# Two half-blocks of an inner layer as steps of their own, and a new table of places for the whole order

## The reference, cut to what matters

```python
x = x + 0.5 * ffn(layernorm(x))
x = x + attention(layernorm(x))
x = x + 0.5 * ffn(layernorm(x))

# ffn, weights ternary: 256 -> 1024 (twice) -> 1024 -> 1024 -> 256
h = silu(lin(x, w1)) * lin(x, w2)
h = gelu(lin(h, h1))
h = gelu(lin(h, h2))
return lin(h, w3)

# attention: 16 heads; each row looks at 24 rows at fixed offsets 0 ... 768 before it
scores = einsum('bhnd,bhnod->bhno', q, k_g) * scale + pos_bias
out = einsum('bhno,bhnod->bhnd', softmax(scores), v_g)
return out_flat * sigmoid(x @ Wgate + bgate) @ Wout + bout
```

## Time and profile before

| | |
|---|---|
| median of 3 runs | 1610.91 us (1610.43 to 1613.33) |
| profiled execution | 1609.98 us, span 1608.1 us |
| PE busy | 1528.4 us (95% of the span) |
| DVE busy | 1086.0 us (68%) |
| ACT busy | 677.6 us (42%) |
| POOL busy | 553.3 us (34%) |
| mean granted TensorE clock | 0.987 |

### The profile page before, as it was taken

The page is one execution under the profiler, slowest core; times in us unless marked ns, Lnnn a source line. Parts: engine busy times, 40 slices in busy tenths (PEclk is TensorE's granted clock), DMA queues, the critical chain, the costliest instruction groups (busy, mean ns, idle before and its releaser), DMA issues.

```text
span 1608.1 us, 19160 instructions
## 1 busy us (share of the span) xinstructions
PE 1528.4 (95%) x6978; PEld 1224.9 (76%) x6978; DVE 1086.0 (68%) x1475; ACT 677.6 (42%) x1062; POOL 553.3 (34%) x402
## 2 busy tenths in 40 slices
PE   7689999999999999999999999999999999998998
PEld 6567888777777778787777877768788877786887
DVE  6323758894777686777876877778675978793322
ACT  7434445344343435344534353434343444352442
POOL 2003051535171607162526070533614245434020
PEclk9899999999999999999999999999999999999999
DMA  7662848666766494857765757557474776754332
GB/s 308 252 241 101 281 140 302 224 207 226 232 234 218 155 312 142 279 171 262 261 229 183 251 182 261 185 192 254 157 265 158 269 247 223 269 198 157 118 100 71
DMA packets 189218, 342.41 MB, mean 213 GB/s; under 512 B 15552, under 2 KB 138560, under 8 KB 188736
## 3 DMA queue, kind: packets, MB, share of 16 engines
q1 hardware_dynamic: 189120, 341.13, 62.1%
HBM read 319.05 MB, written 30.41 MB: 217 GB/s over the span
## 4 chain that ended last, share of the span: by engine, by line
PE 66%; DVE 12%; POOL 8%; DMA 7%; ACT 4%; issue 3%; SPq 0%; DVEq 0%; POOLq 0%; ACTq 0%
PE f_bank L1101 22%; PE f_bank L1102 22%; PE a_banks L1179 6%; PE f_bank L1030 4%; PE f_bank L1031 4%; DMA weights_hi<-in_ffn_w 3%; POOL acc L693 3%; PE f_bank L1130 2%; PE f_bank L1131 2%; DVE slot L935 2%; DVE slot L979 2%; DVE S L941 2%; POOL acc L690 2%; PE a_banks L1199 1%; POOL h_lo L707 1%
## 5 line engine op out<-in xcount | busy, mean ns | idle before, releaser
L1101 PE MATMUL f_bank<-h_hi,wring 128*128 128x512 f32 x2048 | 824.4, 403 | 31.1 <-POOL h_lo L707 12.4
L1102 PE MATMUL f_bank<-h_lo,wring 128*128 128x512 f32 x2048 | 813.6, 397 | 0.0
L1101 PEld LDWEIGHTS f_bank<-h_hi,wring 128*128 128x128 f32 x2048 | 387.6, 189 | 131.9 <-issue 18.4
L1102 PEld LDWEIGHTS f_bank<-h_lo,wring 128*128 128x128 f32 x2048 | 387.6, 189 | 93.2 <-issue 1.4
L773 ACT ACTIVATE h_hi<-f_bank,colv 128x512 fp32r<-128x512 f32 x256 | 176.5, 689 | 553.1 <-PE f_bank L1102 552.9
L895 DVE TENSOR_TENSOR h_lo<-f_bank,h_hi 128x512 fp32r<-128x512 f32 x256 | 175.2, 687 | 258.5 <-ACT f_bank L774 256.8
L707 POOL TENSOR_TENSOR h_lo<-f_gated,h_hi 128x512 fp32r<-128x512 f32 x128 | 165.4, 1305 | 449.1 <-ACT h_hi L767 448.3
L1030 PE MATMUL f_bank<-fT_hi,w_in 128*128 128x512 f32 x480 | 197.5, 411 | 11.6 <-ACT f_gated L762 5.4
L1031 PE MATMUL f_bank<-fT_lo,w_in 128*128 128x512 f32 x480 | 191.5, 399 | 0.0
L979 DVE TENSOR_TENSOR slot<-slot,a_banks 128x1280 f32<-128x1280 f32 (+4 forms) x124 | 169.5, 1375 | 21.1 <-DMA slot<-keys_and_values 20.7
L935 DVE TENSOR_TENSOR slot<-slot,a_banks 128x1280 f32<-128x1280 f32 (+4 forms) x124 | 170.5, 1375 | 17.0 <-DMA slot<-keys_and_values 16.8
(11 more groups left out here) (117 smaller groups left out, 1328.1 us busy)
## 6 DMA issues: line engine op xcount, KB each, us to landing
wring<-weights_hi SPq DMA_DIRECT2D x256, 512.0 KB, 4.6
slot<-keys_and_values SPq DMA_DIRECT2D x128, 384.0 KB, 4.9
slot<-keys_and_values SPq DMA_DIRECT2D x64, 640.0 KB, 4.0
slot<-keys_and_values SPq DMA_DIRECT2D x312, 128.0 KB, 4.4
slot<-keys_and_values SPq DMA_DIRECT2D x64, 256.0 KB, 5.7
weights_hi<-in_ffn_w SPq DMA_DIRECT2D x16, 512.0 KB, 5.0
keys_and_values<-kv_out SPq DMA_DIRECT2D x32, 256.0 KB, 2.3
xf<-in_x SPq DMA_DIRECT2D x8, 512.0 KB, 5.8
```

The costliest lines, as they stand in the source:

```text
L1101: pe.matmul(bank[:, :], hi, h_hi[src][:, k, :], start=(k == 0), stop=False)
L1102: last = pe.matmul(bank[:, :], hi, h_lo[src][:, k, :], start=False, stop=(not general and k == KH - 1))
```

## The change

h(l,0) and h(l,1) are split into four steps: `f_begin` 0 and 1 (turns 0 to 5 of block 0, of block 1) and `f_hidden` 0 and 1 (turns 6 and 7). The matmuls and their order among each other stay as they were; an attention step may now stand at any of the three seams where before it had to stand in front of or behind h(l,0). As the plan of h(l,1) now begins with its `f_begin`, its weight block and, in pass 0, the copy of it are due 3.7 earlier in planned time. And the numbers of the table are new: six of the 14 `TIMES`, most of `FOLLOW`, ten of the 16 `STARTS`.

```diff
-TIMES = [4.5, 9.5, 11.8, 13.4, 16.0, 24.8, 22, 3.8, 5.6, 53.0, 58.4, 3.1, 87.5, 3.5]
+TIMES = [3.5, 9.5, 11.8, 14.3, 16.9, 29.3, 21.6, 3.8, 5.6, 53.0, 58.8, 3.1, 88.4, 3.8]
-FOLLOW = dict(silu=-1.5, gate=0.1, cut=1.9, low=2.0, gelu=-0.6,
-              lo=0.9, residual=-1.3, residual2=0.4, fill=20.7, stats=-0.6, turn=4)
+FOLLOW = dict(silu=-1.5, gate=0.1, cut=1.9, low=2.7, gelu=-1.0,
+              lo=1.0, residual=-0.9, residual2=0.1, fill=23.1, stats=-0.7, turn=4)
-STARTS = [70, 149, 219, 312, 386, 453, 537, 617,
-          688, 768, 847, 925, 1006, 1087, 1158, 1236]
+STARTS = [73, 149, 219, 312, 381, 448, 537, 618,
+          690, 769, 851, 918, 1007, 1087, 1158, 1236]
...
+    ABREAST = 2
...
                 for layer in range(2):
+                    for m in range(ABREAST):
+                        pe(2.8, "f_begin", r, layer, m)
                     for m in range(KH):
-                        done = pe([6.5, 0.95, 3.7][min(m, 2)], "f_hidden", r, layer, m)
+                        done = pe(0.95 if m < ABREAST else 3.7, "f_hidden", r, layer, m)
+                        if m < ABREAST:
+                            begin["f_hidden", r.j, layer, m] = begin["f_begin", r.j, layer, m]
...
-                if general or m > 1:
-                    part(m, 0, KH)
-                elif m == 0:
-                    part(0, 0, EARLY)
-                    part(1, 0, EARLY)
-                    part(0, EARLY, KH)
+                if general:
+                    if not early:
+                        part(m, 0, KH)
+                elif early:
+                    part(m, 0, EARLY)
                 else:
-                    part(1, EARLY, KH)
+                    part(m, EARLY if m < ABREAST else 0, KH)
```

More of the change, by code:

```diff
@@ L1082, in bank_free, with run_hidden @@
                     pe.wait_ge(f_tlo, r.at(2, m - TURN_AT - 1))
-            def run_hidden(r, layer, m, ring, general):
+            def run_hidden(r, layer, m, early, ring, general):
                 src = (r.p + layer) % 2
@@ L1207, in run @@
                     "f_in": lambda r, m: run_in(r, m, ring, general),
-                    "f_hidden": lambda r, layer, m: run_hidden(r, layer, m, ring, general),
+                    "f_begin": lambda r, layer, m: run_hidden(r, layer, m, True, ring, general),
+                    "f_hidden": lambda r, layer, m: run_hidden(r, layer, m, False, ring, general),
                     "f_out": lambda r: run_out(r, ring, general),
```

## The result

| | before | after |
|---|---|---|
| median | 1611.01 us (20 runs, 1606.67 to 1614.85) | 1615.07 us (20 runs, 1609.43 to 1620.78) |
| profiled execution | 1609.98 us, span 1608.1 | 1611.20 us, span 1609.4 |
| mean granted clock, profiled | 0.987 | 0.990 |

The ratio is 1.0027, interval 1.0016 to 1.0038: the change made the kernel 4 us slower. The prediction said 1601, faster, with 1612 as its upper end.

A forecast was written before the change was run, and what follows sets the result against it. It took TensorE's own work, unchanged, plus its stands to bound the kernel. Gains less the losses in passes 5 and 10 summed to -9.5 us, giving 1601 us; own range 1596 to 1607, 8 in 10 for 1593 to 1612.

The forecast's parts named there:

- Pass 11, f_in: In pass 11's f_in, s11 starting earlier removes TensorE's 2.80 us stand and the lower clock behind it: -4.3 us.
- Pass 0, weight blocks: In pass 0, copies 8 and 9 go out together, fill 9 leaves 3.4 us earlier, all kept: -3.4 us.
- Waits for `a_hat`: TensorE's waits for `a_hat` shrink because `stats` is planned 1.0 earlier against `turn`: -2.8 us.
- Pass 9, layer 1: At h(1,4), TensorE comes 1.5 us later and f_lo(1,2) is done 0.8 earlier, ending stand and lower clock: -3.6 us.
- DVE's `h_lo` in passes 4, 5 and 10: TensorE's remaining waits for DVE's layer 1 input in these passes go: -2.4 us.
- Pass 10, layer 0: POOL's sums and `f_low` end later, TensorE stands 4.6 us before `a_z_turn` with lower clock after: +4.1 us.
- pass 5: In layer 0, the same pattern as pass 10 with s4 and s5, including one lower clock stretch: +3.5 us.
- Pass 6: One TensorE wait for `a_z` goes, as s5 starts 5 earlier: -0.6 us.
- Clock: After each long TensorE stand the granted clock falls to its lower level, charged at 1.6 us per stand.
- `a_stats` among the products: Rival: between products 3 and 4 in passes 5 and 10, `a_stats` costs 4.9 us each; about 1611, chance 0.17.
- SP's queue: Rival: earlier fills hold up key and value loads, 1.2 us in each of 13 attention passes; 1616, chance 0.18.
- The seam is free: Rival: sums in passes 5 and 10 start no later, so both loss terms fall away; -17.1, 1594 us, chance 0.17.

The follow-up runs named there:

- lo12_ahead: Changed kernel with DVE's f_lo(1,2) planned 1.7 us earlier; 1611.95 us, ratio to before 1.0007.
- gate_back: Changed kernel with the gate projection back at 24.8 us after a subblock's start instead of 29.3; 1612.52 us, ratio to before 1.0017.
- all_stands_out: Changed kernel with f_lo(1,2) 1.7 us earlier, in passes 4 and 9 its gelu and f_lo another 2.8, s11's statistics 2 us later; 1608.65 us, ratio 0.9987.
- stats_back: Changed kernel with the planned time of stats back from 3.5 to 4.5; 1616.54 us, ratio to before 1.0043.
- s4s5_back: Changed kernel with the starts of s4 and s5 back at 386 and 453; 1615.61 us, ratio to before 1.0034.
- copy_back: Changed kernel with copy 9 in pass 0 put back behind fill 8; 1616.09 us, ratio to before 1.0039.
- stats11_later: Changed kernel with the statistics of s11 planned 2 us later; 1614.23 us, ratio to before 1.0028.
- stats11_and_low2: Changed kernel with s11's statistics planned 2 us later and f_low 2 of pass 10 planned 0.3 us earlier; 1615.45 us, ratio to before 1.003.
- s10_back: Changed kernel with the start of s10 back at 847 instead of 851; 1618.5 us, ratio to before 1.0039.

## Why the prediction was wrong, by its own steps

*Pass 11, f_in (-4.3).* Right: -4.8 in the changed kernel, -4.6 with s11's start alone.

*Pass 0, weight blocks (-3.4).* The mechanism was right: the second fill went out 1.23 us behind the first (1.20 was said). The sum's "they are kept" failed: -1.8 in the profile. The 3.6 us at fill 10 are down to 1.8 at fill 15, as each later copy took longer from its issue to the fill. The experiments put the pair at 1 to 3 us.

*Waits for `a_hat` (-2.8, beside s11's 2.0).* They fell from 6.1 to 2.5 us, by 3.6 of the 4.8. But the step priced only what left. The operation moved is DVE's `a_stats`, and what it is moved past was not looked up: in passes 2 and 12 it went ahead of f_lo(1,2), and h(1,4) stood 1.25 and 2.23 us. lo12_ahead got this back, 3.1 us.

*Pass 9, layer 1 (-3.6), and DVE's `h_lo` in passes 4, 5 and 10 (-2.4).* This is the step that failed most. They said that no wait for DVE's `h_lo` would be left; 9.4 us are, a miss of 9.4 us in the sum. "f_lo(1,2) is done 0.8 us earlier" was read off DVE's order alone. f_lo needs the gelu, and that stands on ScalarE behind `a_tanh` and f_scale, since the gate moved to 29.3; gate_back and all_stands_out show it. Counted from the start of layer 1 in pass 9, TensorE did come to h(1,4) later, by 1.9 us (1.5 was said for the gate's work), but f_lo(1,2) began 1.8 us later too, and the stand went from 2.04 to 1.91 us. Pass 9's 1.8 us in the profile are luck: the half clock of 3.4 us that followed before did not follow. With the four long stands of h(1,4) out, all_stands_out is 6.4 us below the changed kernel, at 0.9987 of before (0.9973 to 1.0001).

*Pass 10, layer 0 (+4.1) and pass 5 (+3.5).* The new stands are where they were said (3.96 us in f_in 6 of pass 10, 2.47 and 2.71 us in f_in of pass 5), but between f_in 0 and layer 1 both passes are only 1.6 us longer in the profile. The reckoning through GpSimd's chain was good to 1.2 us, with T as there the start of pass 10's f_in: the first sum began at T + 3.2 (3.8 was said), `f_low` 7 ended at T + 32.7 (33.9), `a_z_turn` came at T + 38.9 (39.8), h(0,3) at T + 44.6 (45.7). POOL was idle for 0.8 us between that first sum and `f_low` 7. What failed is the clock's part, 1.6 us charged behind a stand of 4.6 us in front of `a_z_turn`. The lower clock came earlier, for 6.8 us in f_in, so TensorE reached that place 2.2 us later than was said and stood 1.52 us instead of 4.6, and its clock stayed at 1.00 behind it. The work lost at half clock was taken out of a wait for POOL. In the five other traces that keep the changed kernel's order of s10's sums (stats_back, s4s5_back, lo12_ahead, copy_back, gate_back) the pass is 1.3 to 3.2 us longer than before up to layer 1, so part of the miss is again the profiled run.

Of pass 10's f_in this much is shown: s10's sums on POOL, 11 us, stand among the `f_low`, and begin 4.8 us later against f_in than before, behind both residuals on DVE. Three other placements (stats11_later, stats11_and_low2, s10_back) bring layer 1 of pass 10 no more than 0.6 us nearer. Before's placement doesn't have these stands; which set of numbers gives it back is open.

*Pass 6 (-0.6).* Right: -0.8 in f_in, where the wait of 0.60 us is gone.

*What was not in the sum:* pass 4 (+3.3 us), pass 2 (+1.4), pass 12 (+2.1), passes 7 and 8 (+1.0 each) and 14 (+0.9). Together they outweigh passes 6, 9 and 11. In pass 4 they are h(1,4)'s 1.96 us, 1.44 in f_in and 0.84 at `a_z_turn`; in pass 7 f_turn stands 1.43 us for f_scale, in pass 8 `a_turn` 1.22 for `a_hat`. Only the places that already stood in before were priced, so every new stand fell outside: the list of TensorE's waits of before can show what a new order may remove, and not what it makes. Which numbers make the other stands of passes 4 and 5 is open; s4's and s5's starts alone don't explain them.

*Clock (1.6 us for each long stand).* Stands of 2 us were charged one lower stretch each. Whether it comes is a matter of the run, below.

*The rivals.* None won, but "`a_stats` among the products" was there. In pass 5 `a_stats` ran 3.0 us and a weighing after it, both in front of product 5, whose silu was done at 544.59; it came at 548.39, and f_in stood 2.71 us for it. In pass 10 `a_stats` of s11 waited 4.29 us for its load and then ran 3.6 us in front of product 4, for which f_in stood 3.96. The same operation held up h(1,4) in pass 12. Its price in time was smaller than the 4.9 us a pass that the rival has, since POOL was late as well. "SP's queue" did not come: DVE waits 18.6 us for values, not more than 20.7. "The seam is free" expected a gain, and 1594 is far off; the split without the table and without the drift costs 0.15%.

## What to carry to other kernels

When every engine runs a fixed order sorted from planned times, price a new table by what each moved step is now in front of, on each engine, and not by the waits of the old profile. A planned cost that changes by 0.05 us cost 2% here, where other steps are placed by absolute times: split or change a step so that the planned sum stays exactly the same, and change places in a second edit. And take such a table apart number by number before taking it whole; here two of its effects, s11's start and one pair of copies, were worth 5.4 us by themselves, and the changed kernel, with everything else beside them, is 9 us slower than the kernel with these two alone.

## What the runs showed of the hardware that was not expected

A stand does not always bring the lower clock, 1.2 GHz instead of 2.4, not even at the same place behind the same wait. In nine kernels with the changed table's order there, TensorE stands 2.23 to 2.25 us in front of h(1,4) of pass 12. In three (the changed kernel, gate_back, copy_back) the clock stayed at full behind it, in six (stats11_later among them) it fell to half for 3.4 us. Windows of the changed kernel and of stats11_later (the clock is the number behind the busy times):

```profile
1297.00:1300.00 3.00, 3.00 (x14) 2.41 (x14) 2.89 (x4) 1.58 (x3) 1.99 (x2) 1.00 0.04 14
```

```profile
1297.00:1300.00 3.00, 3.00 (x8) 2.32 (x8) 2.90 (x4) 1.57 (x3) 1.98 (x2) 0.50 0.06 19
```

Behind the 1.91 us of the changed kernel's pass 9 the clock stayed at 1.00, where before's 2.04 us in the same place were followed by half clock; behind its 3.96 us of pass 10 it was at half for 6.8 us (windows of before, then of the changed kernel):

```profile
1001.00:1004.00 3.00, 3.00 (x9) 2.32 (x8) 2.96 (x5) 0.00 (x0) 0.00 (x0) 0.50 0.91 359
```

```profile
1004.50:1007.50 3.00, 3.00 (x15) 2.41 (x14) 2.97 (x3) 0.18 (x1) 0.00 (x0) 1.00 0.69 239
1041.00:1044.00 3.00, 0.00 (x0) 0.00 (x0) 2.93 (x8) 0.00 (x0) 2.84 (x4) 0.94 1.07 382
1044.60:1047.60 3.00, 3.00 (x8) 2.32 (x9) 3.00 (x3) 2.37 (x4) 2.92 (x5) 0.50 0.23 74
```

A single profiled execution can flatter such a kernel by 4 us. How far the runs of a kernel lie apart doesn't follow from the number of its stands: 11.4 us for the changed kernel (20 runs), 2.2 for lo12_ahead (12 runs) with two stands less, 9.1 for all_stands_out (12 runs) with still fewer. That is open.

The same `a_stats` took 1.6 us in pass 2 and 3.8 in pass 12, the difference in one operation on 128x2 that took 0.16 us there and 2.32 here. What sets it can be read from the traces. In the 17 traces no operation of VectorE on 128x2 that began while GpSimd did nothing took longer than 0.17 us. 390 took over 0.5 us; all of them began during an operation of GpSimd, and each ended 0.01 to 0.03 us after the end of one. So where such a small operation is held up, its length is set by the end of an operation of GpSimd, up to 2.8 us here, and the place to look for its price is POOL's timeline, not its size. In the prediction's rival the 2.32 us of pass 10 before are of this kind.
